# Value products copied by ScalarE, the value bias added behind the product with the probabilities

## The reference

```python
v = (hidden_states @ Wv + bv)                  # 64 tokens x 256 channels, 8 heads of 32
probs = softmax(where(mask, q @ k.T / sqrt(32), -inf))
out = probs @ v                                # 16 query heads, two to each value head
out = out.reshape(..., 512) @ Wo + bo
```

## Time and profile before

| | |
|---|---|
| median of 3 runs | 2649.65 us (2643.26 to 2651.69) |
| the profiled execution | 2647.59 us |
| its span, first to last instruction | 2646.0 us |
| mean granted clock of TensorE | 0.991 of full speed |
| DVE busy | 1982.4 us, 75% of the span |
| ACT busy | 876.3 us, 33% of the span |

### The profile page before, as it was taken

The page is one execution under the profiler, slowest core; times in us unless marked ns, Lnnn a source line. Parts: engine busy times, 40 slices in busy tenths (PEclk is TensorE's granted clock), DMA queues, the critical chain, the costliest instruction groups (busy, mean ns, idle before and its releaser), DMA issues.

```text
span 2646.0 us, 38647 instructions
## 1 busy us (share of the span) xinstructions
PE 2562.0 (97%) x13824; PEld 2162.5 (82%) x13824; DVE 1982.4 (75%) x3052; ACT 876.3 (33%) x1498; POOL 977.0 (37%) x1189
## 2 busy tenths in 40 slices
PE   5899999999899999999999999999999999999999
PEld 5788888888778888888888888888888888888887
DVE  6888888888588888888888888888655454545544
ACT  4445545455332222222222222222222222222222
POOL 3554444535355555564555546555400000000000
PEclk8999999999999999999999999999999999999999
DMA  4232332323789887886688568865557434574562
GB/s 123 73 109 97 98 106 90 109 84 100 273 323 356 318 331 275 319 317 222 239 304 326 217 233 310 322 237 214 223 203 255 186 147 183 192 266 175 189 253 104
DMA packets 167376, 562.26 MB, mean 212 GB/s; under 512 B 21784, under 2 KB 81048, under 8 KB 134560
## 3 DMA queue, kind: packets, MB, share of 16 engines
q1 hardware_dynamic: 131872, 458.10, 47.7%
q0 software_dynamic: 35328, 101.82, 10.2%
HBM read 427.27 MB, written 132.51 MB: 212 GB/s over the span
## 4 chain that ended last, share of the span: by engine, by line
PE 84%; DVE 8%; ACT 4%; issue 2%; DMA 1%; POOL 0%; DVEq 0%; SPq 0%; ACTq 0%; POOLq 0%
PE down L893 26%; PE bank_a L876 26%; PE bank_b L876 13%; PE proj L697 7%; PE bank_c L876 6%; ACT k_diagonal L980 2%; PE scores L738 2%; DVE rope_sin L1223 2%; DVE rope_in L1222 2%; DVE rope_sin L1220 1%; DVE rope_in L1225 1%; PE proj L708 1%; PE pv L764 1%; DMA h_scratch<-h_out 1%; ACT rope_in L966 1%
## 5 line engine op out<-in xcount | busy, mean ns | idle before, releaser
L893 PE MATMUL down<-d_slot,inter_parts 128*128 128x512 f32 x3072 | 737.4, 389 | 0.0
L893 PEld LDWEIGHTS down<-d_slot,inter_parts 128*128 128x128 f32 x3072 | 576.8, 188 | 119.6
L1103 ACT ACTIVATE copy_p<-bank_a 128x512 f32<-128x512 f32 x384 | 229.6, 598 | 744.6 <-PE bank_a L876 744.6
L1411 DVE TENSOR_TENSOR acc<-down,acc 128x512 f32<-128x512 f32 x512 | 349.4, 686 | 67.0 <-PE down L893 59.7
L876 PE MATMUL bank_a<-h_ahead,gu_slot 128*128 128x512 f32 x1536 | 390.2, 389 | 2.4 <-ACT copy_p L1103 1.4
L876 PE MATMUL bank_a<-h_once,gu_slot 128*128 128x512 f32 x1536 | 390.0, 389 | 1.5 <-ACT copy_p L1103 1.5
L876 PEld LDWEIGHTS bank_a<-h_ahead,gu_slot 128*128 128x128 f32 x1536 | 288.1, 188 | 63.5 <-ACT copy_p L1103 2.2
L876 PEld LDWEIGHTS bank_a<-h_once,gu_slot 128*128 128x128 f32 x1536 | 288.2, 188 | 62.0 <-ACT copy_p L1103 2.3
L578 POOL TENSOR_TENSOR lut_v<-lut_v,signed_scale 128x512 f32<-128x512 f32 x96 | 125.2, 1304 | 427.1 <-DVE lut_v L1193 426.4
L1396 DVE TENSOR_TENSOR up<-gate,up 128x512 f32<-128x512 f32 x256 | 209.8, 819 | 91.5 <-ACT gate L1113 77.6
L1120 ACT ACTIVATE inter_parts<-up 128x512 fp32r<-128x512 f32 x256 | 160.6, 630 | 261.8 <-PE down L893 171.1
(11 more groups left out here) (123 smaller groups left out, 3545.8 us busy)
## 6 DMA issues: line engine op xcount, KB each, us to landing
gu_slot<-w_scratch SPq DMA_DIRECT2D x128, 1792.0 KB, 7.6
d_slot<-d_scratch SPq DMA_DIRECT2D x64, 1024.0 KB, 9.6
w_scratch<-w_parts POOLq DMA_DIRECT2D x96, 512.0 KB, 7.5
h_ahead<-h_scratch SPq DMA_DIRECT2D x36, 1024.0 KB, 12.5
h_scratch<-h_out SPq DMA_DIRECT2D x32, 896.0 KB, 5.0
h_once<-h_scratch SPq DMA_DIRECT2D x27, 1024.0 KB, 7.4
acc<-out SPq DMA_DIRECT2D x18, 1024.0 KB, 5.5
out<-acc SPq DMA_DIRECT2D x18, 1024.0 KB, 12.4
```

The lines of the kernel that those rows point to most:

```text
L893: ins = pe.matmul(bank[:], inter_parts[:, j, u, q, e * P:(e + 1) * P], d_slot[m % 2][:, j, part, :], start=(j == 0 and i == 0), stop=(j == ...
L1103: act.activation(copy[:], bank_a[n % 2][:], ACT.Copy).then_inc(copied, 1)
L1411: dve.tensor_tensor(acc[:, q, e], down[turn % 4][:], acc[:, q, e], ALU.add).then_inc(acc_added, 1)
```

## The change

The value product is copied to SBUF by ScalarE without its bias, at the head of ScalarE's iteration. The bias is added where `pv` is read: `heads_high` becomes two activations with a bias per partition (one for each group of heads, 256 columns each), `heads_low` two `scalar_tensor_tensor` (add the bias, subtract the high part). The constant `bv` is loaded as 128 x 2 numbers instead of 256 numbers broadcast to 128 partitions.

```diff
-            bv = sb("bv", [P, 256], F32)
+            bv = sb("bv", [P, 2], F32)
...
-            sp.dma_start(bv[:], a["bv"].to_broadcast([P, 256])).then_inc(const_ld, 16)
+            sp.dma_start(bv[:], a["bv"]).then_inc(const_ld, 16)
...
+            def value(it, q):
+                bank = full_wait(act, it, f"v{q}")
+                act.activation(v_sb[:, q].rearrange("p g d -> p (g d)"), bank[:, 0:256], ACT.Copy).then_inc(proj_free[BANK[f"v{q}"]], 1)
+
             def heads_high(t, q):
                 act.wait_ge(pv_full, t * NP + q + 1)
-                act.activation(attnT[:, HI].rearrange("p k n -> p (k n)"), pv[:].rearrange("p g r b c -> p (g r b c)"), ACT.Copy).then_inc(pv_hi, 1)
+                for gc in range(2):
+                    ins = act.activation(attnT[:, HI, 2 * gc:2 * gc + 2].rearrange("p k n -> p (k n)"),
+                                         pv[:, gc].rearrange("p r b c -> p (r b c)"), ACT.Identity, bias=bv[:, gc:gc + 1])
+                ins.then_inc(pv_hi, 1)
...
             def iteration(t, par, do_tail=True, do_head=True):
                 it = t
+                value(it, 0)
+                value(it, 1)
                 if do_tail:
                     rows_high(t - 1, 1)
...
-            def value(it, q):
-                bank = full_wait(dve, it, f"v{q}")
-                dve.tensor_tensor(v_sb[:, q].rearrange("p g d -> p (g d)"), bank[:, 0:256], bv[:], ALU.add).then_inc(proj_free[BANK[f"v{q}"]], 1)
-
             def heads_low(t, q):
                 dve.wait_ge(pv_hi, t * NP + q + 1)
-                dve.tensor_tensor(attnT[:, LO].rearrange("p k n -> p (k n)"), pv[:].rearrange("p g r b c -> p (g r b c)"),
-                                  attnT[:, HI].rearrange("p k n -> p (k n)").bitcast(F32), ALU.subtract).then_inc(pv_used, 1)
+                for gc in range(2):
+                    hi, lo = (attnT[:, u, 2 * gc:2 * gc + 2].rearrange("p k n -> p (k n)") for u in (HI, LO))
+                    ins = dve.scalar_tensor_tensor(lo, pv[:, gc].rearrange("p r b c -> p (r b c)"), bv[:, gc:gc + 1], hi.bitcast(F32),
+                                                   ALU.add, ALU.subtract)
+                ins.then_inc(pv_used, 1)
...
                 if do_tail:
                     rows_low(t - 1, 1)
-                value(it, 0)
-                value(it, 1)
                 softmax_shift(t, 0)
...
-        "bv": get("L0_attn_bv")[None, :],
+        "bv": get("L0_attn_bv").reshape(2, P).T,
```

## The result

The changed kernel takes 2652.19 us (median of 20 runs, 2647.72 to 2659.24), the kernel before 2645.56 us in its 20 runs (2641.87 to 2652.36). The ratio is 1.0022, with a 95% interval of 1.0014 to 1.0031: slower by 5.8 us, between 3.7 and 8.2. The 5.8 us lie inside 0.3% (7.9 us) and the time inside the predicted range, but the loss is three times the +2 us of the sum.

The account below looks back on a forecast made before the run. Token stage bound by TensorE, then a ScalarE-VectorE relay; heads_high 1.6 and heads_low 0.35 us, the rest 0, sum to 1.95, about +2 us: 2649.6 on the profiled execution, 2651.6 on the median, given as 2651; range 2643 to 2660 us.

Parts of the forecast that it names:

- the sum: All instruction terms together: 0 + 0 + 0 + 1.6 + 0.35 = 1.95 us slower, said as +2 us.
- What bounds the kernel, and the values: Token stage: TensorE, then a ScalarE-VectorE relay, bound it; value-bias additions off VectorE gain 0, since it waits for scores.
- Rival 2: VectorE was the limit after all: 8.4 us gained and 2 lost, 2643 us; chance 0.10.
- the cover of the copies: Head of iteration: two value copies, 0.76 us, fit ScalarE's 2.14 us idle time before the turned rows; cost 0.
- heads_high, second half: On the relay ahead of the query biases: the split pair holds them 0.12 us longer, 13 tiles, 1.6 us.
- heads_low: VectorE's subtraction split in two: 0.05 us more in 7 tiles, 0.35 us, between 0 and 1.5.
- The "tie": Second half of a tile: VectorE's pair and the query biases both end about 458.1; could add up to another 0.1 us.
- The clock: TensorE's clock gate runs freely against the kernel: spread around the forecast, not a shift of it; no term in the total.
- rival 1: TensorE's clock falls more often, four more falls: 7.6 to 10.4 us slower, 2657 to 2660 us; chance 0.11.
- The sign I gave for it: Undisturbed iterations stay and the number of slow score groups moves by four or more.
- the bounds of +1 to +6: Lower and upper limits in us around the forecast's +2 us.
- The base: Time the +2 us was added to: profiled execution 2647.59 us, or a median 2.1 us higher; forecast nearer the median.

Follow-up runs that it names:

- a1: Changed kernel with heads_high and heads_low whole as before, value bias left out, values still copied by ScalarE: 2648.58 us, ratio 1.0001 to the kernel before.
- b1: Kernel before with TensorE's second value product made twice and heads_high alone split in two activations: 2645.00 us, ratio 0.9993.
- b2: Kernel before with TensorE's second value product made twice and heads_low alone split in two scalar_tensor_tensor: 2644.99 us, ratio 0.9988.
- a4: Changed kernel with TensorE's second value product made twice in each iteration but the first: 2645.89 us, ratio 0.9993 to the kernel before.
- a3: Kernel before with TensorE's second value product made twice in each iteration but the first: 2643.68 us, ratio 0.9982.
- c3: Kernel before with two tiny activations (128 x 32) in front of the second heads_high, nothing split: ratio 1.0017, 4.5 us slower.
- c1: Kernel before with one tiny activation (128 x 1) in front of the second heads_high, nothing split: ratio 1.0000.
- c4: Kernel before with three tiny activations (128 x 32) in front of the second heads_high, nothing split: ratio 1.0014, 3.7 us slower.
- b4: Changed kernel with the first two query biases ahead of the second heads_high and heads_low behind the second rope: 2654.38 us, ratio 1.0028.
- b3: Kernel before with the first two query biases ahead of the second heads_high and heads_low behind the second rope: 2647.16 us, ratio 0.9995.

## Why the prediction was right or wrong

- **What bounds the kernel, and the values.** Right. The wait grew by 11.7 us over 16 tiles, a1 measured 0 within its interval. Rival 2 (VectorE the limit after all) is refuted by a1, and the cover of the copies held: 1.59 us of idle time are left.
- **heads_high, second half.** Right: 0.73 us against a forecast of 0.75. Its term was 1.6 us; by the undisturbed iterations of b1 it is 13 x 0.09 = 1.2 us. The estimate of 0.28 us per tile by the Trainium skill ("ScalarE: Activation LUTs", section "What ACT_TABLE_LOAD costs") would have made 3.6 us. The pair does end 0.24 us later (0.84 against 0.60), near the page's figure, but its successor starts only 0.10 us later, as the rows before said.
- **heads_low.** Mis-sized. I priced the new form by the tensor_tensor of the same shape and got 0.05 us. It is 0.18 us (0.79 against 0.61), and each of the pair lasts 477 ns instead of 414. With it the term of 7 tiles is 1.3 us instead of 0.35; b2 has 1.3 us by the medians, but with intervals wider than the term. The row of line 1193 that I priced it by is one instruction of 512 columns with an immediate and no PSUM operand or bias pointer, and didn't show the new form. The "tie" that I named at the second rope came out against VectorE: its pair now ends last in all of tiles 2 to 14. The rope starts 0.10 us later than before, no more than heads_high alone makes it, so the two didn't add up there.
- **Sum.** Instructions alone: forecast 1.95 us, measured 1.8 us in the iterations of the two traces and 2.2 to 2.9 us in a4 against a3.
- **The clock.** This is the step that failed: a term put at nothing. I held it to be scatter around the forecast, after the rule of the Trainium skill that the gate runs freely against the kernel ("TensorE: Matmul & The Clock Gate", Part 1), and gave a shift a chance of 0.11. The runs agree with the scatter: before's own 35 runs beside a1 to a4 lie 12.0 us apart, and filling the idle time brings that to 3.3 in a3 and 3.4 in a4. But there is a shift as well. About 3 of the 5.8 us are this (0.9 to 5.4), and c3 pays 4.5 us for 1.3 us of delay. It is rival 1 in kind and less in size: I had it at four more falls and 7.6 us or more. The sign I gave for it, slow score groups that move by four or more, was not met by the pair of traces (four before, five after), and was too coarse to see a shift of this size. That 5.8 us still lie inside the bounds of +1 to +6 is luck: those bounds were set by pairs that might not overlap, and the rows showed that they do; no part of them stood for the clock.
- **The base.** Adding to the median of three runs, 2649.65, put the forecast at 2651. With 20 runs the median before is 2645.56, so the distance to 2652.19 is 6.6 us, and the good hit of 2651 is in part luck.

## What to carry to other kernels

Work taken off an engine is worth nothing where that engine then waits for another, as VectorE did here for the scores; read what ended the idle time in front of the next instruction before counting busy time. An instruction split in two on the path costs what it delays the start of the next one, so look for a pair of the same form, the same operands and the same pointers, not only of the same size. Where a small idle time of TensorE recurs in each iteration, allow for a longer iteration to cost more than its own length, and try filling the gap: here 12 useless matmuls per iteration gave the kernel before 4.1 us and made up for the change (a4, ratio 0.9993 to the kernel before).

## What the hardware showed that I had not expected

- A tiny activation can be free. In c1 one of 128x1 (0.20 us) stands ahead of heads_high, and the iteration is as long as without it, 40.70 us: from its start to that of heads_high it is 0.11 us, and from there to the successor 0.48 us, 0.59 us together. In c3, timeline:

```profile
373.19 0.35 ACT L1058 ACTIVATE idle<-cos 128x32 f32<-128x32 f32 x2
373.45 0.58 ACT L999 ACTIVATE attnT<-pv 128x512 fp32r<-128x512 f32 x1
373.92 0.83 ACT L967 ACTIVATE rope_in<-proj,bq 128x256 f32<-128x256 f32 x2
```

  Here heads_high lets its successor start after 0.47 us; directly behind the copies of k_place, which cover 32 partitions, it was 0.63. So how soon the next activation follows depended on what stood ahead, in all 15 tiles of c1, c3 and c4. Which property does it was not tried.
- An idle time of 2.48 us on TensorE was followed by half clock and one of 2.32 us was not (b4 and b3), and 1.6 us led to either. Without an idle time over 0.25 us no score group of tiles 2 to 14 was slow (a3, a4). In these traces the idle time is a condition for the fall and not its measure.
